# Cross attention's value product with the values as stationary operand, four heads side by side on 32 array columns each

## The reference

```python
q = (x @ q_w + q_b).reshape(B, N, H, hd).transpose(0, 2, 1, 3)
kv = (cond @ kv_w + kv_b).reshape(B, condN, 2, H, hd)
k = kv[:, :, 0].transpose(0, 2, 1, 3)
v = kv[:, :, 1].transpose(0, 2, 1, 3)
attn = jnp.einsum('bhnd,bhmd->bhnm', q * scale, k)
attn = jax.nn.softmax(attn, axis=-1)
out = jnp.einsum('bhnm,bhmd->bhnd', attn, v)
out = out.transpose(0, 2, 1, 3).reshape(B, N, C)
return out @ proj_w + proj_b
```

## Time and profile before

| | |
|---|---|
| median of 3 runs | 1280.93 us (1279.38 to 1281.05) |
| profiled execution, its time | 1280.48 us |
| its span (first to last instruction) | 1278.7 us |
| PE busy | 1194.4 us, 93% |
| DVE, POOL, ACT busy | 830.7, 729.6, 642.2 us |
| `PV` (L922) matmuls | 3072 |
| `TT` (L928) matmuls | 64 |

### The profile page before, as it was taken

One profiled execution on the slowest core, in us unless ns is written; L12 is line 12 of the kernel. 1 busy time (PEld: TensorE's weight loads), 2 busy tenths in 40 slices (PEclk: granted clock), 3 DMA queues, 4 the chain that ended last, 5 costly groups with the idle time before them and its releaser, 6 DMA issues.

```text
span 1278.7 us, 43327 instructions
## 1 busy us (share of the span) xinstructions
PE 1194.4 (93%) x19120; PEld 806.8 (63%) x19120; DVE 830.7 (65%) x1455; ACT 642.2 (50%) x946; POOL 729.6 (57%) x690
## 2 busy tenths in 40 slices
PE   4789899999999999999999999999999877699997
PEld 4456576767667676767676767676767555555543
DVE  4658476858585867676767777677777586423156
ACT  4335556556565656565656464646565535533300
POOL 1436656667676766667675857575757455500042
PEclk9799999999999999999999999999999988799999
DMA  8010611010202010101011110101010345455356
GB/s 302 2 42 2 240 44 50 3 59 3 66 4 65 17 44 9 53 17 52 19 50 32 38 48 12 43 17 52 17 58 11 116 159 190 146 159 170 131 163 212
DMA packets 47840, 93.28 MB, mean 73 GB/s; under 512 B 3775, under 2 KB 15351, under 8 KB 47655
## 3 DMA queue, kind: packets, MB, share of 16 engines
q1 hardware_dynamic: 44135, 79.03, 18.7%
q0 software_dynamic: 3520, 11.47, 2.9%
HBM read 60.13 MB, written 30.36 MB: 71 GB/s over the span
## 4 chain that ended last, share of the span: by engine, by line
PE 86%; DVE 4%; DMA 3%; POOL 3%; ACT 2%; issue 1%; another core or an unknown queue 1%; SPq 1%; ACTq 0%; DVEq 0%
PE psum L323 56%; PE psum L922 7%; PE psum L1025 6%; PE psum L1010 5%; PE psum L940 2%; PE psum L899 2%; PE psum L891 1%; DMA bank<-in_L_attn_Wv 1%; DMA out<-bank 1%; PE psum L967 1%; PE psum L855 1%; PE psum L907 1%; DVE xT L1176 1%; POOL bank L1444 1%
## 5 line engine op out<-in xcount | busy, mean ns | idle before, releaser
L1444 POOL TENSOR_TENSOR bank<-prob,bank 128x1200 f16<-128x1200 f32 x128 | 314.6, 2468 | 188.4 <-ACT bank L1120 188.3
L1268 DVE TENSOR_REDUCE c_most<-psum 100x4 f32<-100x1444 f32 x128 | 211.6, 1653 | 14.7 <-PE psum L1010 12.6
L323 PE MATMUL psum<-bank,cT 128*128 128x512 f16 (+1 forms) x864 | 198.7, 379 | 0.1
L323 PE MATMUL psum<-cT,bank 128*128 128x361 f16 x1152 | 196.1, 321 | 0.0
L1111 ACT ACTIVATE prob<-psum 128x1200 f32<-128x1200 f32 x128 | 150.0, 1172 | 76.6 <-PE psum L1025 62.4
L1176 DVE TENSOR_TENSOR cv<-psum,cv 128x512 f16<-128x512 f32 x125 | 86.0, 688 | 107.4 <-ACT cv L1102 57.2
L1120 ACT ACTIVATE bank<-prob 128x1200 f16<-128x1200 f32 x128 | 151.7, 1198 | 1.4
L323 PEld LDWEIGHTS psum<-cT,bank 128*128 128x128 f16 x1152 | 106.1, 99 | 65.5 <-DVE c_raw L1195 3.0
L323 PEld LDWEIGHTS psum<-bank,cT 128*128 128x128 f16 (+1 forms) x864 | 85.1, 101 | 88.2 <-issue 4.1
L1102 ACT ACTIVATE cv<-psum 128x512 f16<-128x512 f32 x96 | 57.4, 598 | 149.9 <-PE psum L323 148.3
L1229 DVE SCALAR_TENSOR_TENSOR bank<-psum,b_part,bank 128x361 f16<-128x361 f32 x128 | 74.4, 592 | 81.1 <-ACT bank L1088 81.1
(11 more groups left out here) (215 smaller groups left out, 1905.8 us busy)
## 6 DMA issues: line engine op xcount, KB each, us to landing
c_raw<-in_ctx SPq DMA_DIRECT2D x16, 960.0 KB
xs_scratch<-y_kept SPq DMA_DIRECT2D x1, 7424.0 KB, 22.8
c_raw<-xs_scratch SPq DMA_DIRECT2D x29, 256.0 KB, 2.7
ys_scratch<-bank SPq DMA_DIRECT2D x29, 256.0 KB, 2.0
bank<-in_L_ffn_expert_w SPq DMA_DIRECT2D x7, 1024.0 KB, 7.7
x_in<-in_x SPq DMA_DIRECT2D x16, 200.0 KB
x_scratch<-x_out SPq DMA_DIRECT2D x16, 200.0 KB
y_kept<-x_scratch SPq DMA_DIRECT2D x10, 256.0 KB, 3.2
```

Of the source, the lines that this page charges most:

```text
L323: last = pe.matmul(out_ap, a(pa), b(pb), start=(i == 0 and j == 0), stop=(i == len(pairs) - 1 and j == 2))
L1268: dve.tensor_reduce(c_most[:, hf], score[0:L, :, 0:HC], AXIS.X, ALU.max).then_inc(max_done, 1)
L1444: pool.tensor_tensor(prob16[o % 2][:, (2 + part) * PT:(3 + part) * PT], prob[:, part], prob16[o % 2][:, part * PT:(part + 1) * PT], ALU.su ...
```

## The change

`PV` loads the values as weights (up to 128 rows of the context by the 32 columns of one head) and streams the probabilities of that head through, 100 columns. Four heads stand on the four 32-column parts of the array, and their outputs on the four quarters of the partitions. Per group these are 3 x 6 x 4 = 72 matmuls for the products and 2 x 6 x 4 = 48 more, with a block of ones as weights, which give each head's sums already repeated over its 32 partitions: 120 in place of 48, written to 200 columns of a bank. The output comes out turned, heads on partitions, so `scale_heads`, `TT` and its split fall away. In their place, per group: DVE takes the reciprocal of 128 x 100 sums, waits for it, and multiplies (`head_out`); ACT copies that to the high part of `tT` (`TH`), POOL makes the low part (`TL`). `TP` waits for `TL3` and moves from step 11 to step 6, behind `SV` (in iteration 14 from step 7 to 5). `TH0` and `TL0` stand at the end of step 10, `TH1` and `TL1` in step 18, `TH2` and `TL2` in step 2, `TH3` and `TL3` in step 4. The ones column of the values is not set any more.

```diff
-    ["MX0", "CX2", "CX3", "rotate_k", "CX4"],
+    ["MX0", "CX2", "CX3", "rotate_k", "CX4", "TH2", "TL2"],
     ["T0a", "exp0a", "CX5", "PV3"],
-    ["T0b", "SS0", "SS1", "exp0b", "shift0", "scale_heads", "max_A1", "CK0"],
+    ["T0b", "SS0", "SS1", "exp0b", "shift0", "max_A1", "CK0", "TH3", "TL3"],
     ["A1", "CK1", "shift1", "CK2"],
-    ["B1", "high0a", "max_B1", "TT", "low0a", "self_exp0", "SV"],
+    ["B1", "high0a", "max_B1", "low0a", "self_exp0", "SV", "TP"],
...
-    ["A2", "max_A2", "self_scale1", "self_exp1", "self_sum1", "SP0", "CV1"],
-    ["B2", "SP1", "self_scale2", "high1a", "self_scale3", "max_B2", "TP", "high1b", "low1a", "SP2", "SP3",
+    ["A2", "max_A2", "self_scale1", "self_exp1", "self_sum1", "SP0", "CV1", "TH0", "TL0"],
+    ["B2", "SP1", "self_scale2", "high1a", "self_scale3", "max_B2", "high1b", "low1a", "SP2", "SP3",
      "CV2", "low1b"],
...
-    ["T3a", "exp3a", "stats_x", "CQ", "norm_x", "high3a"],
+    ["T3a", "exp3a", "stats_x", "CQ", "norm_x", "high3a", "TH1", "TL1"],
...
-    ["B1", "max_B1", "low0b", "scale_heads", "FW22", "FW23"],
+    ["B1", "max_B1", "low0b", "TP", "FW22", "FW23"],
     ["MX1", "SC3", "FW30", "FW31"],
-    ["T1a", "exp1a", "SC4", "TT", "FW32"],
+    ["T1a", "exp1a", "SC4", "FW32"],
     ["T1b", "exp1b", "high1a", "PV0", "FW33", "FW40"],
-    ["A2", "max_A2", "low1a", "high1b", "TP", "FW41"],
+    ["A2", "max_A2", "low1a", "high1b", "FW41", "TH0", "TL0"],
...
-END_EXTRA = {2: ["PV3", "scale_heads"], 5: ["TT"], 6: ["TP"], ...
+END_EXTRA = {1: ["TH2", "TL2"], 2: ["PV3"], 3: ["TH3", "TL3"], 5: ["TP"], ...
...
-                for c in range(HT):
+                for a, (pv, pp) in enumerate(((0, 0), (0, 1), (1, 0))):
                     for t in range(CT):
-                        r = CLAST if t == CT - 1 else CW
-                        for p in range(2):
-                            at = ((p * 2 + t // 3) * HT + c) * 3 * L + t % 3 * L
-                            last = pe.matmul(f[:, c * HV:(c + 1) * HV], prob16[i % 2][0:r, at:at + P],
-                                             cv[odd][0:r, t, HT * i + c, 0:HV],
-                                             start=t + p == 0, stop=t + p == CT)
-            elif name == "TT":
-                pe.wait_ge(c_out_done, it.n)
-                for k in range(KD):
-                    last = pe.transpose(f[:, k * L:(k + 1) * L], c_out[:, k * P:(k + 1) * P], ident[0:L, 0:L])
+                        for c in range(HT):
+                            p, r = tile(pp, t, c)
+                            last = pe.matmul(f[DH * c:DH * (c + 1), 0:L], cv_half[odd][0:r, t, HT * i + c, pv], p,
+                                             start=a + t == 0, stop=a == 2 and t == CT - 1)
+                for pp in range(2):
+                    for t in range(CT):
+                        for c in range(HT):
+                            p, r = tile(pp, t, c)
+                            last = pe.matmul(f[DH * c:DH * (c + 1), L:2 * L], ones16[0:r, 0:DH], p,
+                                             start=pp + t == 0, stop=pp == 1 and t == CT - 1)
...
+        def act_head_high(act, it, g):
+            n = it.n - 1 if f"TH{g}" in TAIL else it.n
+            act.wait_ge(chunk_out, (its[n + 1] if g == GROUPS - 1 else its[n]).done(f"PV{g}"))
+            act.activation(tT[:, 0, g], head_out[g % 2][:], ACT.Copy).then_inc(head_high, 1)
...
-                dve.tensor_reduce(c_out[:, HT * DH * i:HT * DH * (i + 1)].rearrange("q (c d) -> q c d", c=HT),
-                                  heads[:, :, 0:2 * DH].rearrange("q c (p d) -> q c d p", p=2), AXIS.X, ALU.add)
-                op = dve.reciprocal(c_rinv[:, HT * i:HT * (i + 1)].unsqueeze(2), heads[:, :, 2 * DH:HV])
+                g = GROUPS * (n - 1 if i == GROUPS - 1 else n) + i
+                dve.reciprocal(head_rinv[:], f[:, L:2 * L]).then_inc(head_inv, 1)
+                dve.wait_ge(head_inv, g + 1)
+                if g >= 2:
+                    dve.wait_ge(head_split, g - 1)
+                op = dve.tensor_tensor(head_out[i % 2][:], f[:, 0:L], head_rinv[:], ALU.mult)
...
+        def pool_head_low(pool, it, g):
+            count = GROUPS * (it.n - 1 if f"TL{g}" in TAIL else it.n) + g + 1
+            pool.wait_ge(head_high, count)
+            pool.tensor_tensor(tT[:, 1, g], head_out[g % 2][:], tT[:, 0, g], ALU.subtract).then_inc(head_split, 1)
```

More of the change, by code:

```diff
@@ L80 @@
     ["MX3", "X2T", "low2b", "PV1"],
-    ["T3a", "exp3a", "stats_x", "CQ", "norm_x", "high3a"],
+    ["T3a", "exp3a", "stats_x", "CQ", "norm_x", "high3a", "TH1", "TL1"],
     ["T3b", "exp3b", "CK7", "split_cq", "PV2", "high3b"],
 ]
-TAIL = ("low3a", "low3b", "PV3", "scale_heads", "TT", "TP")
-CROSS = tuple(f"{w}{g}" for w in ("A", "B", "max_A", "max_B", "MX") for g in range(GROUPS)) + ("PV0", "PV1", "PV2") + tuple(
+TAIL = ("low3a", "low3b", "PV3", "TH2", "TL2", "TH3", "TL3", "TP")
+CROSS = tuple(f"{w}{g}" for w in ("A", "B", "max_A", "max_B", "MX") for g in range(GROUPS)) + ("PV0", "PV1", "PV2", "TH0", "TL0", "TH1", "TL1") + tuple(
     f"{w}{g}{p}" for w in ("T", "exp", "high", "low") for g in range(GROUPS) for p in "ab" if w != "low" or g < GROUPS - 1)
-CHUNKS = ("X1T", "X2T", "SQ", "SK", "CQ", "SV", "SO", "OP", "TT", "TP")
+CHUNKS = ("X1T", "X2T", "SQ", "SK", "CQ", "SV", "SO", "OP", "TP")
 CHUNK_KINDS = ("CX", "CK", "CV", "SS", "SP", "MX", "PV", "BV", "FX", "FG", "FW", "FL", "FR", "ST")
@@ L142 @@
 ]
-END_EXTRA = {2: ["PV3", "scale_heads"], 5: ["TT"], 6: ["TP"], 9: ["FS12"], 10: ["FN12"], 11: ["FX12"], 12: ["FL12"],
+END_EXTRA = {1: ["TH2", "TL2"], 2: ["PV3"], 3: ["TH3", "TL3"], 5: ["TP"], 9: ["FS12"], 10: ["FN12"], 11: ["FX12"], 12: ["FL12"],
              13: ["RT10", "RE1"], 14: ["RT11"], 15: ["RT12"], 16: ["RT13"]}
@@ L153, in steps_of @@
         return END_STEPS
-    every = [list(step) for step in (moved(STEPS, "TP", 7) if n == B - 2 else STEPS)]
+    every = [list(step) for step in (moved(STEPS, "TP", 5) if n == B - 2 else STEPS)]
     for t in range(EARLY - 1):
@@ L162, in steps_of @@
     return every
-SPLIT = ("X1T", "SV", "SP0", "SP1", "SP2", "SP3", "SO", "X2T", "TT") + tuple(
+SPLIT = ("X1T", "SV", "SP0", "SP1", "SP2", "SP3", "SO", "X2T") + tuple(
     [f"MX{g}" for g in range(GROUPS)] + [f"CX{c}" for c in range(6)] + ["FG0"] + [f"FW{e}{k}" for e in range(E) for k in range(KD)] + [f"FX{t}" for t in range(TILES)] + [f"CK{c}" for c in range(8)] + [f"CV{c}" for c in range(6)] +
@@ L284, in build_layer @@
         max_sign, max_second, minus = sb("max_sign", [P, 1]), sb("max_second", [P, 1]), sb("minus", [P, P], F16)
-        c_rinv = sb("c_rinv", [L, H])
-        c_out = sb("c_out", [L, D])
+        head_rinv, head_out = sb("head_rinv", [P, L]), [sb(f"head_out{i}", [P, L]) for i in range(2)]
         psum = stack.enter_context(nc.psum_tensor("psum", [P, 8, BANK], F32))
@@ L996, in pe_scores @@
                 pe.wait_ge(k_padded, 1)
[L997 removed]
+                pe.wait_ge(place_consts, PLACE_CONSTS)
                 pe.wait_ge(prob_padded, 2)
@@ L1039, in pe_iteration @@
                         pe_slots(pe, int(name[2:]))
-                    elif name[0] == "T":
+                    elif name[0] == "T" and name[1].isdigit():
                         pe_turned_scores(pe, it, int(name[1]), "ab".index(name[2]))
@@ L1472, in pool_iteration @@
                         pool_norm(pool, x_norm[0], x_in[:], 2 * m + 2)
-                    elif name == "scale_heads":
-                        pool_heads_scale(pool, it)
+                    elif name[:2] == "TL":
+                        pool_head_low(pool, it, int(name[2]))
                     elif name[:2] == "FN":
```

36 lines of the change are left out of this document (19 added, 17 removed).

## The result

The changed kernel takes 1375.0 us (median of 4 runs, 1372.8 to 1385.2), the kernel before 1281.0 on the same chip: a ratio of 1.075, interval 1.070 to 1.081. That is 94 us more, where 23.5 were forecast. The direction was right, the size wrong by a factor of four, and the time lies far above the range. The profiled execution took 1374.0 with a span of 1372.2.

A forecast was written before the change was run, and what follows sets the result against it. PE was taken as the bound, with 86% of the chain that ended last. Step 11 25.9, iterations 0 and 14 1.8, SQ 3.5, TT -5.7, other products -2.0 gave +23.5 on 1280.48: 1304.0 us, range 1290 to 1317.

The forecast's parts named there:

- the value product on PE: PV's 120 matmuls at SO's spacing take 1.52 us against 1.56 before; 64 products: -2.5 us, from -7 to +6.
- The matmuls side by side: PV's matmuls overlap, 10.9 ns apart; rival without overlap: 32 ns each, 1458 us, chance 0.02; skill's 25 ns: some 1400.
- Step 11: Without TP's cover SP2 and SP3 wait for POOL's pair, which TL0 delays: 1.99 us an iteration, 25.9 over iterations 1 to 13.
- Rival 1: In step 11 POOL's pair is not held by TL0, or by neither: 1.07 to 1.65 us an iteration, 1290 to 1298, chance 0.14.
- TT: Four transposes leave PE in iterations 1 to 14 and at the end: 15 x -0.38 = -5.7 us.
- SQ: SQ waits longer for DVE's split of X1T, behind PV2's reciprocal and multiply: 0.25 us, 14 times, 3.5 us.
- The clock: Rival: idle in step 11 brings 1.2 GHz, 1.7 us each time; with a slower DVE 1311 to 1330, chance 0.12 together.
- Iterations 0, 14 and 15: 0 and 14 already wait, so lose only the pair's 0.92 less PV0's gain, 0.88 us each; 15 taken as 0, within 2.

The follow-up runs named there:

- e2: The changed kernel with TP back in step 11 and TH0 and TL0 at the end of step 12: 1344.9 us, ratio 1.050.
- e7: e2 with all its 12000 columns a product in 72 matmuls in place of 120, DVE adding both pairs of halves: 1324.8 us, ratio 1.034.
- e9: e6 with the sum of the halves written to free columns of the PSUM bank in place of SBUF: 1286.1 us, ratio 1.005.
- e11: e9 with 48 matmuls more in each product, the ones against 16 columns, which nothing reads: 1352.9 us, ratio 1.056.
- e3: The changed kernel with only TH0 and TL0 moved to the end of step 12, TP staying in step 6: 1365.8 us, ratio 1.066.
- e4: e2 with PV0 behind SP1, PV1 between CV4 and CV5, PV3 between CK1 and CK2: 1353.6 us, ratio 1.059.
- e6: e2 with 72 matmuls a product, ones against the high part alone, DVE adding the two halves into SBUF before the multiply: 1312.3 us, ratio 1.024.

## Why the prediction was right and wrong

*What failed: the value product on PE.* The prediction costed it by the array: `SO`'s spacing of 10.9 ns times 120, so 1.45 to 1.65 us, 1.52 taken. Where nothing stops it, that is right; `PV0` and `PV3` of the changed kernel show it (next operation at 603.20 and 581.97, 1.48 and 1.49 us after the start):

```profile
580.48 1.00 PE L925 MATMUL psum<-bank,cv 128*32 128x100 f16 x72
...
581.30 0.73 PE L931 MATMUL psum<-bank,ones 128*32 128x100 f16 x48
...
581.97 0.31 PE L1032 MATMUL psum<-cq,bank 32*128 32x100 f16 x12
```

The step left out that the instructions have to arrive. `SO` was the right row for the array and the wrong one for the supply: its 96 instructions pass in 0.66 us, and with the turned score ahead of it they are 192 in 1.29, just as dense, but long matmuls stand on both sides. `PV3` stands between two turned scores and three transposes; together they now hold 438 instructions in 3.1 us, where there were 294. Between 160 and 1010 us the densest 256 instructions of PE in a row take 1.52 us in the changed kernel and 2.82 in the kernel before. A term for this would have been such a count of instructions over time from the same timelines. Its price is 45.0 us of idle time, and more in busy time. From e2 to e7 the same columns in 72 matmuls save 40 us of issue and only 20 of time, because PE's waits for DVE grew from 34.3 to 63.0. From e9 to e11 the 48 matmuls cost 67 us in all.

*The matmuls side by side: right.* A floor of 25 ns for each, one after the other, as the prediction worked it out from the Trainium skill (TensorEngine Tiling (Array Packing), Instruction Overhead), did not show: 120 took 1.49 us, 12.4 ns each.

*The supply itself.* The kernel before had no stop over 0.5 us between 160 and 1010 us, the changed one 31. The Trainium skill, Runtime: NRT & Kernel Launch, Instruction fetch mechanics, says that an engine's instructions are streamed in blocks of 256 and that crossing a block is "mostly hidden": the trace agrees on the size (all stops at one place in a count by 256) and, for the kernel before, on the cover; for the changed kernel it disagrees.

*Step 11: right.* Forecast 13 x 2.03 of wait, 26.4; measured 23.0 (`SP1` to `SP2` 16.9, `SP2` to `SP3` 6.1). Against `SP1`, POOL's pair starts 0.73 us later than before, where 0.92 was taken. The parts were near too: `TL0` 0.375 us for 0.40, `TH0` 0.277 for 0.30, multiply 0.262 for 0.29. e3 and e2 show the two halves of the mechanism, `TL0` ahead of the pair and the lost cover. Rival 1's price for the bare cover, 1.07 to 1.65 us, holds in e3: 2.12 - 1.07 = 1.05 in two iterations, some 1.45 in ten. What the prediction read as POOL's wait ahead of `SP2` in iteration 0 was, by its row, a wait for DVE's split of `CV1`, and in e3 it is that again.

*TT: right,* -5.2 of -5.7 in iterations 1 to 13.

*SQ: wrong, mis-sized.* Forecast +0.25 us each time; in iteration 7 PE waits 0.36 for DVE's split of `X1T`, as before:

```profile
571.03 0.78 DVE L1275 RECIPROCAL head_rinv<-psum 128x100 f32<-128x100 f32 x1 [1.28 <-PE psum L931]
571.52 0.50 ACT L1080 ACTIVATE xT<-psum 128x400 f16<-128x400 f32 x1 [1.30 <-PE psum L854]
571.85 0.26 DVE L1279 TENSOR_TENSOR head_out<-psum,head_rinv 128x100 f32<-128x100 f32 x1
572.05 0.57 DVE L1191 TENSOR_TENSOR xT<-psum,xT 128x400 f16<-128x400 f32 x1
...
572.77 2.30 PE L322 MATMUL psum<-xT,bank 128*128 128x100 f16 x48 [0.36 <-DVE xT L1191]
```

The row of before says that DVE stood idle 0.40 us for ACT's copy ahead of the split; that was the slack. Reciprocal and multiply take 1.02 us to the next instruction, not 1.19, since the reciprocal lasts 0.78 and not 0.90 (the line through the smaller pair of rows gave 0.81), and `PV2`'s result comes 0.1 us sooner against `X1T`. So DVE is free for the split at 572.05, just when ACT's copy has ended (572.02).

*The clock: in part.* Three of the 13 iterations fell to the lower level behind step 11, as that rival described; the first (length, busy us of PE, PEld, DVE, ACT, POOL, granted clock):

```profile
263.50:269.50 6.00, 4.57 (x46) 2.38 (x43) 5.93 (x9) 3.60 (x7) 2.46 (x5) 1.00 0.02 4
269.50:272.90 3.40, 3.40 (x11) 1.68 (x12) 2.07 (x4) 1.54 (x3) 3.40 (x2) 0.50 0.02 5
```

PE idled 1.4 of 6 us and was then granted 1.2 GHz for 3.4. At 1.7 us each that is 5 us, within the rival's price. It is not step 11 alone: in e2_tp11, which has no wait there, four of these iterations fell to the lower level, each within 1.5 us of the end of a stop. Over the whole span PE's busy time at the lower level rose from 42.6 to 69.2 us; at half the speed that is some 13 us, an estimate, of the 23.7 by which its busy time rose.

*Left out besides.* Operations ahead of a product take 0.09 us longer (1.2 us over 13 iterations each at `CX5`, `X2T` and `CK7`); that the change of the array's shape is what costs it is not shown. Iterations 0, 14 and 15 lost 6.7, 8.6 and 7.7 us, forecast 0.9, 0.9 and 0; of these some 3, 6 and 1 are stops, and in iteration 15 some 5 us are new waits that were not followed up. Where a packet comes too late follows from the count: in every kernel here the packets between 160 and 1010 us began with at most 294 of PE's instructions left ahead of the place where it would stop, so PE runs dry where these pass sooner than the 2.2 to 2.9 us from a packet's start to the next matmul. What makes a packet begin, and what passes in the 1.2 to 1.6 us from its landing to the next matmul, no run shows.

## What to carry to other kernels

Before an operation is cut into more and shorter instructions, count the engine's instructions over time, neighbours included, and compare the densest few hundred in a row with the densest that run without stops now (here 256 in 1.52 us against 2.82); array time alone is a lower end. When an operation moves, ask what it was covering in its old place: that question priced `TP` rightly, and forgetting it lost e4. When an intermediate result moves from PSUM to SBUF, look at what POOL does beside the instruction that reads it.

## What the runs showed of the hardware

Between 160 and 1010 us PE's stops for want of an instruction, those of over 0.5 us, all stood at one place in a count by 256: 31 of 31 in the changed kernel, 155 of 155 in the eleven of the experiments, each 2.2 to 2.9 us after a packet of instructions began.

Forty-eight matmuls of 16 columns, whose results nothing reads, cost 1.05 us a product where they crowd with others (67 us by 64 products), and some 0.26 of it is their own time. This was not expected in any term of the sum.

A multiply of DVE with both operands in SBUF that started beside POOL's low part ended only behind it: 0.26 us became 0.56 to 2.33, 17 times in e6, each ending 0.12 us after POOL's. With one operand in PSUM none of 64 took over 0.27. The Trainium skill, SBUF — State Buffer, SBUF: two separate sides, says this of DVE instructions with two SBUF inputs against POOL; the traces agree.
